# A memory stage that takes in its gate scan, applies decay and drift on rows, and moves its last norm to ScalarE

## What is computed

```
q = l2norm(xc @ q_w.T)
eta   = sigmoid(mlp(xc, eta_w1, eta_w2)).mean(batch, features)       # one number per step
alpha = sigmoid(mlp(xc, alpha_w1, alpha_w2)).mean(batch, features)
for t in steps:                    # carried: w1, w2, started at mem_w1, mem_w2
    o[t] = q[t] + gelu(q[t] @ w1) @ w2
    w1 = w1 * alpha[t] - eta[t] * 0.01
    w2 = w2 * alpha[t] - eta[t] * 0.01
h = h + o
z = layernorm(h)                   # goes to the experts; logits = z @ gate_w
```

## Time and profile before

| | |
|---|---|
| median of three runs | 4164.19 us (4160.98 to 4185.65) |
| the profiled execution | 4193.22 us, span 4191.4 us |
| busy in the span: TensorE, its weight loads | 3591.3 us (86%), 2764.9 us |
| busy: VectorE, GpSimd, ScalarE | 2534.1 us (60%), 2256.9 us (54%), 1868.7 us (45%) |
| first memset of the gate phase, of the memory phase, of the tail | 3229.43, 3237.08, 3492.19 us |
| mean granted clock of TensorE | 0.943 of 2.4 GHz |

### The profile page before, as it was taken

The page is one execution under the profiler, slowest core; times in us unless marked ns, Lnnn a source line. Parts: engine busy times, 40 slices in busy tenths (PEclk is TensorE's granted clock), DMA queues, the critical chain, the costliest instruction groups (busy, mean ns, idle before and its releaser), DMA issues. The chain is left out here.

```text
span 4191.4 us, 92430 instructions
## 1 busy us (share of the span) xinstructions
PE 3591.3 (86%) x30906; PEld 2764.9 (66%) x30906; DVE 2534.1 (60%) x6578; ACT 1868.7 (45%) x3340; POOL 2256.9 (54%) x2633
## 2 busy tenths in 40 slices
PE   8779999879999879999878999886887887876973
PEld 8757777667777657777656777763333665655763
DVE  1246776557776546777546777555775887865211
ACT  0036666336666435666534666542332443311331
POOL 0065663566664466666365666354554663264776
PEclk9879999999999989999998999998999998997997
DMA  6556664036666025666114666300000223131342
GB/s 222 162 106 122 126 127 92 3 72 127 125 125 117 8 53 109 123 126 127 37 36 89 122 126 125 72 1 28 22 22 20 57 64 48 35 87 41 65 63 29
DMA packets 456034, 341.81 MB, mean 82 GB/s; under 512 B 70659, under 2 KB 440171, under 8 KB 455595
## 3 DMA queue, kind: packets, MB, share of 16 engines
q1 hardware_dynamic: 413635, 314.62, 36.4%
q0 software_dynamic: 27136, 16.42, 2.9%
q10 hardware_dynamic: 15008, 7.51, 0.7%
HBM read 227.69 MB, written 109.29 MB: 80 GB/s over the span
## 5 line engine op out<-in xcount | busy, mean ns | idle before, releaser
L720 DVE TENSOR_REDUCE a_neg_max<-a_S 99x4 f32<-99x788 f32 x1024 | 1003.7, 980 | 560.3 <-PE a_S L351 546.5
L533 ACT ACTIVATE a_probs<-a_St 99x792 f32<-99x792 f32 (+1 forms) x1024 | 850.3, 830 | 683.5 <-PE a_St L368 671.9
L368 PE MATMUL a_St<-a_q_st,a_k_st 99*99 99x198 bf16 (+1 forms) x4096 | 530.1, 252 | 84.4 <-DMA a_q_st<-a_max_rows 70.2
L351 PE MATMUL a_S<-a_k_st,a_q_st 96*99 96x197 bf16 x4096 | 551.9, 258 | 45.7 <-DVE a_neg_max L720 45.5
L351 PEld LDWEIGHTS a_S<-a_k_st,a_q_st 96*99 96x99 bf16 x4096 | 399.5, 128 | 266.8 <-DVE a_neg_max L720 221.5
L368 PEld LDWEIGHTS a_St<-a_q_st,a_k_st 99*99 99x99 bf16 (+1 forms) x4096 | 391.5, 126 | 116.7 <-DMA a_q_st<-a_max_rows 69.6
L385 PE MATMUL a_O<-a_probs,a_v_aug 99*32 99x198 f32 (+1 forms) x8192 | 464.5, 339 | 0.4
L663 POOL TENSOR_TENSOR h<-h,a_rows 99x512 f32<-99x512 f32 x128 | 162.5, 1270 | 277.3 <-DVE a_m_xn L801 277.3
L385 PEld LDWEIGHTS a_O<-a_probs,a_v_aug 99*32 99x32 f32 (+1 forms) x8192 | 246.6, 110 | 84.7 <-issue 2.1
L631 POOL CAST a_max_parts<-a_neg_max 99x32 bf16<-99x32 f32 x128 | 26.8, 209 | 471.8 <-DVE a_neg_max L720 471.8
L512 PEld LDWEIGHTS a_O<-a_w,a_gelu 128*99 128x99 f32 x2048 | 241.7, 168 | 45.5 <-issue 29.2
(11 more groups left out here) (267 smaller groups left out, 7473.8 us busy)
## 6 DMA issues: line engine op xcount, KB each, us to landing
xpatch<-in_x SPq DMA_DIRECT2D x64, 594.0 KB, 3.7
spill_q<-a_parts SPq DMA_DIRECT2D x384, 99.0 KB
spill_k<-a_parts SPq DMA_DIRECT2D x384, 99.0 KB
a_k_st<-spill_k SPq DMA_DIRECT2D x128, 297.0 KB
a_q_st<-spill_q SPq DMA_DIRECT2D x128, 297.0 KB
a_k_st<-spill_k SPq DMA_DIRECT2D x128, 198.0 KB
a_q_st<-spill_q SPq DMA_DIRECT2D x128, 198.0 KB
a_k_st<-spill_k SPq DMA_DIRECT2D x128, 99.0 KB
```

Of the source, the lines that this page charges most:

```text
L351: mm = nc.tensor.matmul(S[0:TC, j // 2, j % 2 * TB:j % 2 * TB + NTOK], q_st[p % 4][0:SPLIT, head, b * TB + c * TC:b * TB + (c + 1) * TC], ...
L368: mm = nc.tensor.matmul(St[0:keys, j // 2, j % 2 * TB:(j % 2 + 1) * TB], k_st[p][:, head, first:first + keys], q_st[p][:, head, b * TB:(b ...
L533: nc.scalar.activation(probs[0:keys, u % 4, :].rearrange("p (x t) -> p x t", x=2), St[0:keys, :, 0:2 * TB], ACT.Exp).then_inc(s["probs"], 1)
L720: nc.vector.tensor_reduce(out.rearrange("p (x y) -> p x y", x=2), S[0:TC, :, 0:2 * TB].rearrange("p x (y t) -> p x y t", y=2)[:, :, :, 0:N ...
```

## The change

`gate_phase` goes; its matmuls, means and scans stand at the head of `memory_phase`, so one clearing of semaphores and one meeting of the engines fall away. The loop is written out for all turns (i from -6) and has other distances between the stages of a pair: the query of pair i+6, its unit query at i+5, transposed and scaled at i+4, `up` and gelu at i+3, `down` at i+2, residual and statistics at i+1, the last norm at i, its transposes at i-1, logits at i-2. `xc` and `zs` are gone: queries and logits read `g.xT`, which is one column wider. The copy of the transposed norm to `g.xT` is made by VectorE.

The gelu goes to `down` as it is. `mem_w2` has a 129th column of -1, so that each row of `Op` carries minus its row sum. VectorE multiplies these sums by the drift of the row (`row_sum`), and ScalarE applies `decay * Op + b` tile by tile into `o` (`weigh`); decay and drift per row come from four small matmuls at i = -3. VectorE adds `o` and `hc`. The last norm is `rstd * h + shift` on ScalarE (`normalise`), with `shift = -mean * rstd` from VectorE (`negate`). The added rows of `hc`, `gel` and others are set by GpSimd. `hc` and `qn` have four buffers, `Qp`, `gel`, `q_decay`, `q_drift`, `mv`, `rstd` two.

```diff
--- before.py
+++ after.py
-        qn = [sb(f"qn{p}", [TL, 4, D]) for p in range(2)]
-        q_decay, q_drift = sb("q_decay", [D, WL]), sb("q_drift", [D, WL])
-        gel = sb("gel", [D, WL])
-        g_decay, g_drift = ([sb(f"{n}{p}", [D, WL + 1]) for p in range(2)] for n in ("g_decay", "g_drift"))
-        hc = [sb(f"hc{p}", [TL, 4, D]) for p in range(2)]
-        stats, mv, ve, rstd = sb("stats", [TL, 4, 6]), sb("mv", [TL, 4, 2]), sb("ve", [TL, 4]), sb("rstd", [TL, 4])
...
+        router, minus, ones = sb("router", [D, E]), sb("minus", [D, D]), sb("ones", [D, D])
+        decay, drift = sb("decay", [D, 2, L]), sb("drift", [D, 2, L])
+        mean, zero, one_step = sb("mean", [D, 2, L]), sb("zero", [D, L]), sb("one_step", [D, L])
...
+        qn = [sb(f"qn{p}", [TL, 4, D]) for p in range(4)]
+        hc = [sb(f"hc{p}", [TL, 4, D]) for p in range(4)]
+        q_decay, q_drift = ([sb(f"{n}{p}", [D, WL]) for p in range(2)] for n in ("q_decay", "q_drift"))
+        gel = [sb(f"gel{p}", [D, WL + 1]) for p in range(2)]
+        b, o = sb("b", [TL, 4]), [sb(f"o{p}", [TL, 4, D]) for p in range(2)]
+        stats, mv, ve = sb("stats", [TL, 4, 6]), [sb(f"mv{p}", [TL, 4, 2]) for p in range(2)], sb("ve", [TL, 4])
+        rstd, shift = ([sb(f"{n}{p}", [TL, 4, 1]) for p in range(2)] for n in ("rstd", "shift"))
...
+        Qp = [ctx.enter_context(nc.psum_tensor(f"y_Q{p}", [128, 512], F32)) for p in range(2)]
+        QTp, Up, ZTp, Lp = (ctx.enter_context(nc.psum_tensor("y_" + n, [128, 512], F32)) for n in ("QT", "U", "ZT", "L"))
+        Op = ctx.enter_context(nc.psum_tensor("y_O", [128, 2, 512], F32))
...
+                sp.dma_start(w_q[:], A["memory_w"][:, 0]).then_inc(s["y_wq"], 16)
+                sp.dma_start(w1[:], A["memory_w"][:, 1]).then_inc(s["y_w1"], 16)
...
+                sp.wait_ge(s["y_set"], 9)
+                for i in range(-LAST, PAIRS + 1):
+                    n = i + 4
+                    if live(n):
+                        wait(sp, s["y_h2"], n - 3)
...
+                            row = n * WL + cols[t]
+                            sp.dma_start(hc[n % 4][0:rows[t], t, :], g.hcat[row:row + rows[t], :])\
+                                .then_inc(hc_in[n % 4], 16)
+                    n = i
+                    if live(n):
+                        wait(sp, s["y_zn"], n + 1)
...
+                def down(n):
+                    wait(pe, s["y_gelu"], n + 1)
+                    wait(pe, s["y_o"], n)
+                    for t in range(4):
+                        mm = nc.tensor.matmul(o_tile(t), gel[n % 2][:, cols[t]:cols[t] + TL], w2[:], start=True, stop=True)
+                    mm.then_inc(s["y_down"], 1)
+
+                def up(n):
+                    wait(pe, s["y_q2"], 2 * (n + 1))
+                    wait(pe, s["y_gelu"], n)
+                    nc.tensor.matmul(Up[:, 0:WL], w1[:], q_decay[n % 2][:], start=True, stop=False)
+                    nc.tensor.matmul(Up[:, 0:WL], minus[:], q_drift[n % 2][:], start=False,
+                                     stop=True).then_inc(s["y_up"], 1)
...
+                def turn_z(n):
+                    wait(pe, s["y_zn"], n + 1)
+                    wait(pe, s["y_zT"], n)
...
+                def turn_q(n):
+                    wait(pe, s["y_qn"], n + 1)
+                    wait(pe, s["y_q2"], 2 * n)
...
+                def logit(n):
+                    wait(pe, s["y_zT"], n + 1)
+                    wait(pe, s["y_lg"], n)
...
+                        mm = nc.tensor.matmul(Lp[0:rows[t], t * E:(t + 1) * E], g.xT[:, at:at + rows[t]], router[:],
...
+                def query(n):
+                    wait(pe, s["y_qn"], n - 1)
+                    for t in range(4):
+                        at = n * WL + cols[t]
+                        mm = nc.tensor.matmul(Qp[n % 2][0:TL, t * D:(t + 1) * D], g.xT[:, at:at + TL], w_q[:],
+                                              start=True, stop=True)
...
+                pe.wait_ge(s["y_ones"], 1)
+                for k in range(2):
+                    for item in range(2):
+                        mm = nc.tensor.matmul(Lp[:, k * L:(k + 1) * L], ones[:], g.gate_sum[:, k, item * L:(item + 1) * L],
+                                              start=(item == 0), stop=(item == 1))
+                    mm.then_inc(s["y_total"], 1)
+                pe.wait_ge(s["y_wq"], 16)
...
+                for i in range(-LAST, PAIRS + 3):
+                    if i == -3:
+                        pe.wait_ge(s["y_scan"], 2)
+                        for k, rowwise in enumerate((decay, drift)):
+                            for c in range(2):
+                                mm = nc.tensor.matmul(ZTp[0:rows[c], 2 * k + c:2 * k + c + 1],
+                                                      rowwise[:, 0, c * TL:c * TL + rows[c]], g.all_mean[:, 0:1],
+                                                      start=True, stop=True)
+                        mm.then_inc(s["y_cols_ps"], 1)
...
+                    if live(i + 2):
+                        down(i + 2)
+                    if live(i + 3):
+                        up(i + 3)
+                    if live(i - 1):
+                        turn_z(i - 1)
+                    if live(i + 4):
+                        turn_q(i + 4)
+                    if live(i - 2):
+                        logit(i - 2)
+                    if live(i + 6):
+                        query(i + 6)
...
+                def normalise(n):
+                    wait(act, s["y_shift"], n + 1)
+                    wait(act, s["y_turned"], n - 1)
+                    wait(act, sent[n % 2], 64 * (n // 2))
+                    for t in range(4):
+                        a = nc.scalar.activation(zn[n % 2][:, t, :], g.h[0:TL, 4 * n + t, :], ACT.Identity,
+                                                 bias=shift[n % 2][:, t, :], scale=rstd[n % 2][:, t, :])
+                    a.then_inc(s["y_zn"], 1)
+
+                def weigh(n):
+                    wait(act, s["y_b"], n + 1)
+                    wait(act, s["y_h2"], n - 1)
+                    for t in range(4):
+                        a = nc.scalar.activation(o[n % 2][:, t, :], o_tile(t)[:, 0:D], ACT.Identity,
+                                                 bias=b[:, t:t + 1], scale=decay_col[:, t % 2:t % 2 + 1])
+                    a.then_inc(s["y_o"], 1)
...
+                def gelu(n):
+                    wait(act, s["y_up"], n + 1)
+                    wait(act, s["y_down"], n - 1)
+                    nc.scalar.activation(gel[n % 2][:, 0:WL], Up[:, 0:WL], ACT.Gelu).then_inc(s["y_gelu"], 1)
...
+                def squares(n):
+                    wait(act, s["y_q"], n + 1)
+                    wait(act, s["y_max"], n)
...
+                for i in range(-LAST, PAIRS + 1):
+                    if live(i):
+                        normalise(i)
+                    if live(i + 2):
+                        weigh(i + 2)
+                    if live(i + 3):
+                        gelu(i + 3)
+                    if live(i + 6):
+                        squares(i + 6)
...
+                def add_q(n):
+                    wait(pool, hc_in[n % 4], 64 * (n // 4 + 1))
+                    wait(pool, s["y_qn"], n + 1)
+                    nc.gpsimd.tensor_tensor(hc[n % 4][:], hc[n % 4][:], qn[n % 4][:], ALU.add).then_inc(s["y_pre"], 1)
...
+                def first_rinv(n):
+                    wait(pool, s["y_sq"], n + 1)
+                    wait(pool, s["y_rinv"], n)
+                    nc.gpsimd.tensor_scalar(ssm[:], ss[:], 1e-24, None, ALU.max).then_inc(s["y_max"], 1)
+                    wait(pool, s["y_max"], n + 1)
+                    wait(pool, s["y_qn"], n)
+                    nc.gpsimd.tensor_tensor(rinv[:, :, 0], ssm[:], g.neg_half[0:TL, 0:1].to_broadcast([TL, 4]),
+                                            ALU.pow).then_inc(s["y_rinv"], 1)
...
+                def second_rstd(n):
+                    wait(pool, s["y_aggr"], n + 1)
+                    wait(pool, s["y_rstd"], n)
...
+                nc.gpsimd.memset(g.xT[:, T:T + 1], 0.0).then_inc(s["y_set"], 1)
+                for p in range(4):
+                    nc.gpsimd.memset(hc[p][:], 0.0).then_inc(s["y_set"], 1)
...
+                for i in range(-LAST, PAIRS):
+                    if live(i + 1):
+                        second_rstd(i + 1)
+                    if live(i + 2):
+                        add_q(i + 2)
+                    if live(i + 6):
+                        first_rinv(i + 6)
...
+                def negate(n):
+                    wait(dve, s["y_rstd"], n + 1)
+                    wait(dve, s["y_zn"], n - 1)
+                    nc.vector.scalar_tensor_tensor(shift[n % 2][:, :, 0], mv[n % 2][:, :, 0], -1.0, rstd[n % 2][:, :, 0],
+                                                   ALU.mult, ALU.mult).then_inc(s["y_shift"], 1)
+
+                def unit(n):
+                    wait(dve, s["y_rinv"], n + 1)
+                    wait(dve, s["y_qT"], n - 3)
```

(75 more changed lines are left out.)

301 lines of the change are left out of this document (80 added, 221 removed).

## The result

The changed kernel takes **4227.27 us** (median of 4 runs, 4222.69 to 4246.61), the kernel before beside it 4169.82 (4160.98 to 4185.65): a ratio of **1.0131** [1.0102, 1.0161]. The forecast was 4176, its range ended at 4216: the change is slower, and by more than the range allowed. The profiled execution took 4225.68 us, its span 4223.9 (4193.22 and 4191.4 before).

A forecast was written before the change was run, and what follows sets the result against it. Bound by the longest way round a turn, 8.05 us, not by engine work: front 7.1 less, fill 16.1, 27 turns 217.4, drain 28.4, semaphores 1.1 sum to +12 us, forecast 4176, range 4150 to 4216.

The forecast's parts named there:

- TensorE's clock falls in its pause: Rival for the memory loop: a 2.9 us pause brings 1.2 GHz, the TensorE way becomes 9.75 us, total 4222; chance 0.15.
- The granted clock of 1.00: Old kernel's steady memory phase: TensorE's clock reading, with pauses like 0.60 us, used as evidence against the falling clock.
- the earlier trace: Layer transposes after TensorE pauses of 2.5 us: 0.56 us once (2.4 GHz) and 0.92 another time (1.2 GHz).
- the sign of being wrong: Steady memory loop: wrong if the unit query does not wait for `rinv`, or TensorE's pause brings the clock under 0.8.
- fill: Start of the memory loop, before the full turns: 16.1 us together, its steps 2.0, 3.6, 4.1 and 6.4.
- drain: End of the memory loop: 28.4 us from the last unit query until the last logits are ready.
- front: Start of the memory phase up to the first unit query, which comes at 3237.9, 7.1 us earlier.
- semaphores: Behind the memory phase: 44 cleared instead of 30, the 14 more taken at 1.1 us.
- The longest way round: Memory loop: unit query over `row_sum`, `weigh`, `gelu`, squares and `rinv` to the next unit query, 8.05 us a turn.
- the way over TensorE: Memory loop: `row_sum`, `weigh`, `gelu`, `down`, `up`, both transposes, scalings and statistics, 8.0 us a turn.
- GpSimd's floor: Memory loop: aggregates to `ve`, GpSimd's whole list, then unit query, 7.6 us a turn even with new instructions free.
- The small scaled copy: ScalarE's `weigh` copies of 128 columns with bias and scale from tiles: 0.34 us a step, 1.36 for four.

The follow-up runs named there:

- experiment 1: Changed kernel plus five idle matmuls in TensorE's pause of each full turn; 4187.19 us, ratio 1.0055 to the kernel before.
- experiment 3: Changed kernel with TensorE transposing the unit query before `down` and `up` instead of behind them; 4179.18 us, ratio 1.0034 to the kernel before.
- experiment 2: Changed kernel with squares and `rinv` first in their lists and queries for pair i+7 instead of i+6; 4225.63 us, ratio 1.0131 to the kernel before.
- experiment 5: experiment 1 with four fillers and `weigh` as plain copies without scale and bias; one run, 4180.72 us against 4182.14 for the kernel before.
- experiment 7: experiment 1 with one filler matmul instead of five in TensorE's pause; one run, 4232.37 us.
- experiment 4: Changed kernel with experiment 2 and experiment 3 together, `up` before `down`, gelu before `normalise` and `weigh`, `rstd` last on GpSimd; 4102.77 us, ratio 0.9836.
- experiment 6: experiment 1 with the last norm back on VectorE in place of `negate`, and `normalise` gone; 4212.18 us, ratio 1.0066 to the kernel before.
- experiment 8: experiment 4 with the last norm back on VectorE in place of `negate`; 4137.04 us, ratio 0.9891 to the kernel before.

## Why the prediction was wrong

**The step that failed** is the choice between forecast and rival under "TensorE's clock falls in its pause": the sum of the forecast puts the clock's cost at nothing. It saw the pause (2.9 us; measured 2.7 to 2.8), priced what follows if it brings the clock down (a way of 9.75, 4222 us), and gave that 0.15. The runs showed matmuls at 1.2 GHz in 21 of 27 turns, a mean turn of 9.41 us instead of 8.05, and 4227 us; with the pause filled (experiment 1) or the matmuls off the way (experiment 3) the turn is 7.95. The reading behind the 0.15 was weak in two places. The granted clock of 1.00 belongs to turns with pauses of 0.60; it said nothing for a TensorE that stands still for a third of each turn. And the earlier trace rows, the only rows with pauses of that length, had the low clock in one of two cases. Those rows alone would have allowed a chance near a half, and a range up to the rival's time. Two bounds were off as well: by the rival's own figures the time is 1% longer from 9.2 us a turn, so from two long turns in three and not three in four; and the sign of being wrong, a clock under 0.8, was not reached at 0.81, where the turn was already 1.4 us too long.

That the rival's 4222 comes so near to 4227 has some luck in it. It had every turn at 9.75, 46 us in all. The turns cost 37 more than forecast, and filling and draining, which it left as they were, 11 more. Nor does every round begin at 1.2 GHz: the clock mostly falls after TensorE has taken up its work again, as the rows above show. The Trainium skill (TensorE: Matmul & The Clock Gate, HAM oscillation) tells of rounds that start cold behind a long wait in each; the waits of its example are longer than the 2.7 us here, and the trace agrees with it in one turn of four (`down` at 2.07 us).

**Mis-sized with it:** fill (+3.3 us) and drain (+7.9). The granted clock was 0.68 in the fill and 0.73 in the drain, where the forecast counted all but the first steps at the high clock; in the fill the miss is its third interval, 6.92 us for 4.1, in which `up` (1.88 and 1.73 us) and the queries (1.81 us) run at the low one. With the turns (+36.8) these are 48 us; front and semaphores give 0.6 back, which leaves the 47 between +12 and +59.

**What was right.** The longest way round, 8.05 against 7.95 to 7.96, shown by experiment 1 and, with the way over TensorE gone, by experiment 3. Experiment 1 makes the clock assumption true in the full turns: 4187 against 4176. Against its own kernel before it is +18.5 us where +12 were forecast; its turns are 1.5 us less than forecast in all, its fill and drain 12 us more. The way over TensorE, 8.0 against 7.84 (experiment 2). GpSimd's floor, 7.6 against 7.38 (experiment 5). The small scaled copy: 0.34 a step forecast, and measured in ScalarE's own rows of the changed kernel:

```profile
3363.57 1.51 ACT L1268 ACTIVATE y_o<-y_O,y_b,y_decay_col 115x128 f32<-115x128 f32 x4 [3.46 <-DVE y_b L1383]
3364.95 0.56 ACT L1275 ACTIVATE y_gel<-y_U 128x458 f32<-128x458 f32 x1
```

1.38 us for four, 0.345 a step, against 0.16 without both pointers in experiment 5: 0.185 for the two, 0.09 each, so the second is paid like the first. The front gave 7.6 of its own where 7.1 were forecast, the semaphores 1.0 of 1.1. That the busy shares decide nothing held too: VectorE fell from 88% to 57%, and the turn grew.

**Left open:** what exactly brings the clock down. The pause right before a turn does not decide it alone: in the changed kernel the same 2.67 us stand before a turn that begins low and one that runs at the high clock. The pauses and the clock of the steady stretch were 2.7 us and 0.81 (the change), 0.36 and 1.66 with 0.88 (experiment 7), 0 to 1.0 and 1.1 to 1.6 with 0.93 (experiment 3), 0.48 with 1.00 (experiment 1). More standing still goes with a lower clock, but these kernels change the length and the share of the pauses together, and they don't tell the two apart. What the other changes of order in experiment 4 (`up`, the gelu, `rstd`) add to the two cuts was not tried apart. The two dropped copies on ScalarE were not tried alone; its idle time of 3.5 us before `weigh` speaks for their being worth nothing.

## What to carry to other kernels

In a pipeline with in-order lists, work out the longest way from each late instruction back to itself one turn later before believing the busy shares; the gain from moving work off a full engine is only had when the lists hand over late results a turn early (here the same work is 1.3% slower in one order and 1.6% faster in another). A way that closes only after two turns counts with half its length. Price every way that passes through TensorE at both clocks as soon as the new order gives TensorE a pause in each turn that the old one did not have, and let single pauses of that length in the old trace weigh in the chance. Where two ways are within a few tenths, removing one shortens the turn only to the other (7.84 and 7.95 here): remove both.

## What was not expected of the hardware

**A tiny instruction of VectorE can last as long as GpSimd's.** `negate` works on 4 elements a row. In the changed kernel it takes 1.22 us, in experiment 4 0.16 (rows above). GpSimd in the changed kernel at that time:

```profile
3363.85 1.01 POOL L1319 TENSOR_TENSOR y_rstd<-y_ve,neg_half 115x4 f32<-115x4 f32 x1
3364.82 1.26 POOL L1301 TENSOR_TENSOR y_hc<-y_hc,y_qn 115x512 f32<-115x512 f32 x1
```

The addition runs from 3364.82 to 3366.08, `negate` from 3364.89 to 3366.11: it ends with it. In experiment 4 `rstd` is the last job of GpSimd's list, and no addition comes right behind it. The Trainium skill (SBUF — State Buffer, SBUF: two separate sides) has VectorE and GpSimd share a port pair that one holds for its whole instruction; the two durations fit. It cost nothing here, since the unit query behind it waited for `rinv` 1.91 us more. The norm shows the same: 2.05 us for four beside the addition (experiment 6, where the first of them takes 1.28 us and ends 0.08 after the addition), 1.12 without (experiment 8). It does so in the kernel before too, where GpSimd's product by drift stands beside it, from 3353.36 to 3354.53. The first of the four norms ends just behind it:

```profile
3353.67 0.94 DVE L1366 TENSOR_SCALAR y_zn<-h,y_mv,y_rstd 115x128 f32 x1 [0.57 <-POOL y_rstd L1309]
```

The median of the 128 is 0.336 us, their mean 0.589. So of the 2.12 us that made the norm look costly about 0.8 lie above what four median ones take, and in the turn shown this is time beside work of GpSimd.

**Adding useless work made a kernel 40 us faster** (experiment 1 against the change): ten matmul instructions of 229 columns a turn, 2.20 us, for 1.46 us less per turn.
